# Selective scan in a two-layer Perceiver block: every second unit scans into SBUF, and TensorE turns its states and sums them through diagonals of C

## The reference, cut to what matters

```
ab = seq @ W_in.T
a, g = jnp.split(ab, 2, axis=-1)
...
a = jax.nn.silu(jnp.swapaxes(y, 1, 2))
B = a @ W_sB.T
C = a @ W_sC.T
s_delta = jax.nn.softplus(D_param + a @ W_sD1.T @ W_sD2.T)
expA = jnp.exp(-A_param)
A_bar = expA[None, None] * s_delta[..., None]
X_bar = B[:, :, None, :] * s_delta[..., None] * a[..., None]
...
    h = At * h + Xt
...
out_ssm = jnp.einsum('lbds,lbs->lbd', hid, jnp.moveaxis(C, 1, 0))
out_ssm = jnp.moveaxis(out_ssm, 0, 1) + D_param * a
out = out_ssm * jax.nn.silu(g) @ W_out.T
```

## Time and profile before

| | us |
|---|---|
| median of 3 runs | 764.37 (764.09 to 766.4) |
| the profiled execution, its own time | 763.98 |
| its span in the trace | 761.8 |
| PE busy | 688.7 (90%) |
| DVE busy | 549.7 (72%) |
| POOL busy | 424.2 (56%) |
| ACT busy | 397.0 (52%) |
| first scan to the last chunk's gating | 586.35 to 704.86 |

### The profile page before, as it was taken

How to read it: one execution, slowest core, us unless ns; L and a number is a source line. 1 busy time by engine, 2 the same in 40 slices (tenths; PEclk the granted TensorE clock), 3 DMA queues, 4 the chain that set the end, 5 groups by cost and what they waited for, 6 DMA issues and landing times.

```text
span 761.8 us, 14840 instructions
## 1 busy us (share of the span) xinstructions
PE 688.7 (90%) x5400; PEld 533.1 (70%) x5400; DVE 549.7 (72%) x1182; ACT 397.0 (52%) x754; POOL 424.2 (56%) x448
## 2 busy tenths in 40 slices
PE   5799999999998879999999999998989677678987
PEld 2577777877776668999999999984553222223677
DVE  5678877877878567067777777427474899998586
ACT  3566756656655333466666666432348655432332
POOL 4638634645637025877887777371123779983130
PEclk9999999999999988999999999999999889989999
DMA  8201101101020289999988989989143600001000
GB/s 337 102 2 57 57 1 55 55 0 55 0 93 19 112 322 383 341 374 416 370 317 328 344 336 341 391 320 396 60 145 109 281 0 1 0 0 42 1 1 28
DMA packets 20952, 125.54 MB, mean 165 GB/s; under 512 B 2288, under 2 KB 6784, under 8 KB 13600
## 3 DMA queue, kind: packets, MB, share of 16 engines
q1 hardware_dynamic: 18016, 116.95, 40.2%
q0 software_dynamic: 2880, 7.87, 2.8%
HBM read 114.00 MB, written 10.81 MB: 164 GB/s over the span
## 4 chain that ended last, share of the span: by engine, by line
PE 71%; DVE 17%; ACT 6%; issue 4%; DMA 1%; POOL 0%; SPq 0%; DVEq 0%; ACTq 0%; PEldq 0%
PE banks L1966 61%; PE banks L2035 8%; DVE banks L1844 6%; DVE shown L1855 1%; DMA ctx_raw<-in_ctxT 1%; ACT probs L1019 1%; DVE negmax_raw L1446 1%; PE banks L2203 1%; DVE stats L1333 1%; ACT ctx_hi L1005 1%; DVE xn L1345 1%; DVE X L1925 1%; DVE X L1715 0%; PE banks L2355 0%; ACT banks L1257 0%
## 5 line engine op out<-in xcount | busy, mean ns | idle before, releaser
L1966 PE MATMUL banks<-xT,raw 128*128 128x128 f32 x992 | 150.7, 275 | 0.6 <-DVE xT L1661 0.6
L1966 PEld LDWEIGHTS banks<-xT,raw 128*128 128x128 f32 x992 | 134.5, 191 | 3.3 <-issue 1.1
L891 POOL TENSOR_TENSOR w_lo<-raw,w_hi 128x1024 fp32r<-128x1024 f32 x48 | 113.2, 2384 | 1.7 <-ACT w_hi L1112 1.0
L1143 ACT ACTIVATE banks<-banks,later 128x128 f32<-128x128 f32 x192 | 65.1, 339 | 53.7 <-PE banks L1966 52.3
L955 POOL TENSOR_TENSOR inject<-BCbc,drive 128x1024 f32<-128x1024 f32 x32 | 75.1, 2354 | 29.4 <-DVE banks L1844 15.2
L1966 PE MATMUL banks<-shown,table 128*128 128x512 f32 x128 | 68.7, 667 | 25.0 <-DVE shown L1855 18.5
L1048 ACT ACTIVATE probsT<-banks 128x512 f32<-128x512 f32 x64 | 38.3, 598 | 86.4 <-PE banks L2035 86.1
L1446 DVE TENSOR_REDUCE negmax_raw<-banks 128x1 f32<-128x1024 f32 x64 | 77.6, 1212 | 3.3 <-PE banks L1966 3.2
L1667 DVE CAST mid_hi<-banks 128x128 fp32r<-128x128 f32 x192 | 55.5, 289 | 32.5 <-ACT banks L1143 30.5
L1019 ACT ACTIVATE probs<-banks,negmax 128x1024 f32<-128x1024 f32 x64 | 71.1, 1111 | 10.9 <-DVE negmax L1448 10.8
L1844 DVE TENSOR_TENSOR_SCAN banks<-banks,inject 128x1024 f32<-128x1024 f32 x32 | 73.2, 2289 | 3.2 <-ACT banks L1257 2.5
(11 more groups left out here) (332 smaller groups left out, 1613.9 us busy)
## 6 DMA issues: line engine op xcount, KB each, us to landing
raw<-in_w SPq DMA_DIRECT2D x31, 2048.0 KB, 9.3
ctx_raw<-in_ctxT SPq DMA_DIRECT2D x8, 1024.0 KB, 4.8
ctxT<-in_ctxT SPq DMA_DIRECT2D x4, 2048.0 KB, 9.6
ctxN<-in_ctxN SPq DMA_DIRECT2D x4, 2048.0 KB, 10.8
BCbc<-bc_rows SPq DMA_DIRECT2D x5, 1024.0 KB, 13.5
x_slots<-zero SPq DMA_DIRECT2D x1, 3968.0 KB, 12.1
y_slots<-y_tile POOLq DMA_DIRECT2D x28, 128.0 KB, 7.0
wf<-in_w SPq DMA_DIRECT2D x9, 384.0 KB, 4.8
```

The costliest lines, as they stand in the source:

```text
L891: nc.gpsimd.tensor_tensor(w2_lo[i % WB][:, cols], raw[i % WB][:, EW // 2:][:, cols], w2_hi[i % 2][:, cols].bitcast(F32), ALU.subtract).the ...
L1143: nc.scalar.activation(to, held, ACT.Gelu, bias=b1[:, bass.ds(at + u, 1)]).then_inc(gelu_done, 1)
L1966: return nc.tensor.matmul(o, lhsT, rhs, start=start, stop=stop)
```

## The change

Units with even g stay as they were ("row units"). Units with odd g ("column units", `by_columns`) go another way:

- DVE scans from the PSUM pair and `inject` into `shown[1]` in SBUF, and does not multiply by C. The scan waits until PE has turned the states of the column unit before (`states_turned`).
- PE turns the states (`turn_states`): eight transposes of 128 x 128 into the pair of banks 4 and 5, which the scan has just left.
- ACT copies both banks into `turned_back` (`take_back`), 128 x 512 each; only then may `decays` write the pair for unit n+2 (`states_back`).
- PE sums with C (`sum_columns`): eight fp32 matmuls of 128 x 128, whose stationary operand is the turned states (tokens on partitions) and whose moving operand is a diagonal matrix with C of those 128 tokens. The product turns the states back to channels and weights them.
- The diagonals are made once, in chunk 0 (`build_diag`): 8 products of the identity and a column of C for each of the four odd g, 32 in all, by DVE, into the part of `Cbc` that the odd units no longer load. The columns of C come from four small matmuls of PE behind the first spread rows, copied by DVE (`c_cols`). The first decays wait for that copy, since it frees bank 0.

Around it: the C halves of the odd units' DMAs are gone (4 x 0.5 MB); the three logarithms and the identity scalings on ACT are spread over g = 3 to 6 and POOL's `step_end` waits for its own logarithm alone; the gate keeps two tiles of `gT`; the gate projection stands behind the first column unit's transposes, and `project_out1` behind the second's.

```diff
-        gT = sb("phase", "gT", [P, CC, TOK])
+        gT = sb("phase", "gT", [P, 2, TOK])
+        turned_back = sb("phase", "turned_back", [P, GS, TC, P])
...
+        def by_columns(g):
+
+            return g % 2 == 1
+
+        def c_diag(g, s, t):
+
+            return Cbc[:, GS * g + s, t * P:(t + 1) * P]
...
-                pool.wait_ge(soft_ready, CC)
+                pool.wait_ge(soft_ready, m + 1)
...
-                if n >= 2:
-                    act.wait_ge(shown_ready, n - 1)
+                if n == 0:
+                    act.wait_ge(cols_ready, cols_before + 1)
                 elif n == 1:
                     act.wait_ge(relu_ready, 2)
+                elif by_columns(g):
+                    act.wait_ge(states_back, cols_before + GS * columns_before(n))
+                else:
+                    act.wait_ge(shown_ready, rows_before(n))
...
+            def take_back(n):
+
+                g = n % GROUPS
+                for s in range(GS):
+                    act.wait_ge(states_turned, turned_before + GS * columns_before(n) + s + 1)
+                    if n >= 2:
+                        act.wait_ge(states_used, cols_before + columns_before(n))
+                    nc.scalar.activation(turned_back[:, s].rearrange("p t n -> p (t n)"), pb(2 * HELD_BANKS[g % 2] + s), ACT.Copy)\
+                        .then_inc(states_back, 1)
...
             for m in range(1, CC):
                 for g in range(GROUPS):
+                    if by_columns(g):
+                        take_back(GROUPS * m + g - 2)
                     decays(m, g)
...
+            def build_diag(g):
+                for s in range(GS):
+                    for t in range(TC):
+                        col = NSTATE + GS * g + s
+                        last = nc.vector.tensor_scalar(c_diag(g, s, t), ident, c_cols[:, t, col:col + 1], None, ALU.mult)
+                last.then_inc(diag_built, 1)
...
             step_part(1)
+            dve.wait_ge(cols_done, cols_before + 1)
+            nc.vector.tensor_copy(c_cols[:].rearrange("p t n -> p (t n)"), pb(LOW_BANK)[:, 0:TC * 2 * NSTATE]).then_inc(cols_ready, 1)
             step_part(2)
+            dve.wait_ge(cols_ready, cols_before + 1)
+            build_diag(1)
...
+                    if by_columns(g):
+                        if n >= 2:
+                            dve.wait_ge(states_turned, turned_before + GS * columns_before(n))
+                        nc.vector.tensor_tensor_scan(shown[g % 2][:].rearrange("p g n -> p (g n)"), held, scan_in,
+                                                     0.0, ALU.mult, ALU.add).then_inc(scanned, 1)
+                        if m == 0 and g + 2 < GROUPS:
+                            build_diag(g + 2)
+                        continue
...
+            def turn_states(m, g):
+                n = GROUPS * m + g
+                pe.wait_ge(scanned, n + 1)
+                for s in range(GS):
+                    for t in range(TC):
+                        last = nc.tensor.transpose(pb(2 * HELD_BANKS[g % 2] + s)[:, t * P:(t + 1) * P], shown[g % 2][:, s, t * P:(t + 1) * P], ident)
+                    last.then_inc(states_turned, 1)
+
+            def sum_columns(m, g):
+                n = GROUPS * m + g
+                if m == 0:
+                    pe.wait_ge(diag_built, cols_before + columns_before(n) + 1)
+                for s in range(GS):
+                    pe.wait_ge(states_back, cols_before + GS * columns_before(n) + s + 1)
+                    for t in range(TC):
+                        last = mm(pb(Y_BANK)[:, t * P:(t + 1) * P], turned_back[:, s, t, :], c_diag(g, s, t),
+                                  False, g == GROUPS - 1 and s == GS - 1 and t == TC - 1)
+                last.then_inc(states_used, 1)
...
-                for g in range(GROUPS):
-                    sum_states(m, g)
-                    if g == 1:
+                for g in range(0, GROUPS, 2):
+                    sum_rows(m, g)
+                    turn_states(m, g + 1)
+                    if g == 0:
                         project_gate(m)
-                    if m and g == 3:
+                    if m and g == 2:
                         project_out1(m - 1, False)
+                    sum_columns(m, g + 1)
```

More of the change, by code:

```diff
@@ L1259, in decays @@
                 last.then_inc(decay_ready, 1)
+            def take_back(n):
[6 more added lines that the diff above has]
+                        .then_inc(states_back, 1)
             def silu_g(m):
                 act.wait_ge(gates_done, m + 1)
-                nc.scalar.activation(gT[:, m, :], pb(GATE_BANK), ACT.Silu).then_inc(g_ready, 1)
+                if m >= 2:
+                    act.wait_ge(gated_ready, m - 1)
+                nc.scalar.activation(gT[:, m % 2, :], pb(GATE_BANK), ACT.Silu).then_inc(g_ready, 1)
             def split_high1(n):
@@ L1268, in split_high1, with scale_ident @@
                 nc.scalar.activation(f_hi[n][:], wf[n][:], ACT.Copy).then_inc(f_hi_ready, 1)
+            def scale_ident(m):
+                nc.scalar.activation(skip_diag[:, m * P:(m + 1) * P], ident, ACT.Copy, scale=part(later, LATER, "d_param")[:, m:m + 1])\
+                    .then_inc(skip_made, 1)
             act.wait_ge(expa_ready, 1)
             for g in range(GROUPS):
+                if g >= 3 and by_columns(g - 2):
+                    take_back(g - 2)
                 decays(0, g)
@@ L1282, in _ @@
                         exp_of_step(m)
-                if g == 2:
+                if 3 <= g < 2 + CC:
+                    log_of_step(g - 2)
+                if g == 5:
+                    scale_ident(0)
+                if g == 6:
                     for m in range(1, CC):
-                        log_of_step(m)
-                    for m in range(CC):
-                        nc.scalar.activation(skip_diag[:, m * P:(m + 1) * P], ident, ACT.Copy, scale=part(later, LATER, "d_param")[:, m:m + 1])\
-                            .then_inc(skip_made, 1)
+                        scale_ident(m)
             silu_g(0)
@@ L1296, in _ @@
                         silu_g(m)
+            take_back(UNITS1 - 1)
             act.wait_ge(x_updated, 5)
@@ L1843, in _ @@
                     dve.wait_ge(inject_ready, n + 1)
-                    nc.vector.tensor_tensor_scan(held, held, inject[g % 2][:].rearrange("p g n -> p (g n)"),
-                                                 0.0, ALU.mult, ALU.add).then_inc(scanned, 1)
+                    scan_in = inject[g % 2][:].rearrange("p g n -> p (g n)")
+                    if by_columns(g):
[5 more added lines that the diff above has]
+                            build_diag(g + 2)
+                        continue
+                    nc.vector.tensor_tensor_scan(held, held, scan_in, 0.0, ALU.mult, ALU.add).then_inc(scanned, 1)
                     dve.wait_ge(scanned, n + 1)
@@ L2442, in _ @@
                 spread_row(0, s)
+            pe.wait_ge(low_ready, 1)
+            for t in range(TC):
+                last = mm(pb(LOW_BANK)[:, t * 2 * NSTATE:(t + 1) * 2 * NSTATE], bc[:, t * P:(t + 1) * P], ident[0:2 * NSTATE, 0:2 * NSTATE],
+                          t == 0, t == TC - 1)
+            last.then_inc(cols_done, 1)
             project_step(2)
@@ L2467, in sum_states @@
                 for s in range(GS):
-                    last = mm(pb(Y_BANK), ident, shown[g % 2][:, s, :], g == 0 and s == 0, g == GROUPS - 1 and s == GS - 1)
+                    last = mm(pb(Y_BANK), ident, shown[g % 2][:, s, :], g == 0 and s == 0, False)
                 last.then_inc(shown_used, 1)
+            def turn_states(m, g):
[11 more added lines that the diff above has]
+                    pe.wait_ge(states_back, cols_before + GS * columns_before(n) + s + 1)
+                    for t in range(TC):
+                        last = mm(pb(Y_BANK)[:, t * P:(t + 1) * P], turned_back[:, s, t, :], c_diag(g, s, t),
+                                  False, g == GROUPS - 1 and s == GS - 1 and t == TC - 1)
+                last.then_inc(states_used, 1)
                 if g == GROUPS - 1:
-                    pe.wait_ge(shown_used, GROUPS * (m + 1))
+                    pe.wait_ge(states_used, cols_before + columns_before(n) + 1)
                     pe.sem_inc(y_ready, 1)
```

20 lines of the change are left out of this document (15 added, 5 removed).

## The result

The changed kernel takes 770.54 us (median of 8 runs, 768.05 to 771.6) beside 764.76 for the kernel before on the same chip: ratio 1.0061, 95% interval 1.0037 to 1.0085. It is slower by 0.6%, little but clear of its interval, and the forecast of 757.5 was wrong in sign. The profiled execution took 769.7 us with a span of 767.9, 6.1 us over the 761.8 of before.

The account below looks back on a forecast made before the run. DVE was taken to bound the scan stage, with POOL becoming the bound in chunks 1 and 2. The terms 1.5 - 2.7 + 0.6 - 3.6 - 2.7 + 0.4 = -6.5 us took 763.98 to 757.5 us, range 754 to 763.5.

Parts of the forecast that it names:

- (a): Start of the scan stage: small matmuls and eight diagonals delay the first scan, +1.5 us.
- (b): Chunk 0, first scan to scan 8: products with C and stalls go, diagonals come in, -2.7 us.
- Rival 3: Chunks 1 and 2: POOL's products slow to 2.5 us beside DVE's scans into SBUF, 760; 0.13 together with Rival 2.
- (d): Chunks 1 and 2, scan 9 to scan 25: POOL becomes the bound, a chunk falls from 28.4 to 26.6, -3.6 us.
- Rival 1: Scan stage: TensorE's clock falls, each pair hit adds 3.5 us; one fall (761) 0.08, two or more (764.5, 768) 0.09.
- (c): Scan 8 to scan 9, with chunk 0's gating: the sum now ends late with a column unit, +0.6 us.
- (e): Chunk 3, scan 25 to scan 31: pairs run at 5.68 us plus 1.0 of holds, 18.1 for 20.78, -2.7 us.
- (f): Tail, last scan to the gating's end: about 6.8 us instead of 6.40, +0.4 us.
- Rival 2: PE-ACT-PE handovers each cost 0.3 us more, delaying column scans and chunk-end sums, +3, 760; 0.13 together with Rival 3.
- rival 4: Scan stage: holds fill DVE's saved product in every pair, which stays near 6.9 us, 764 to 766; chance 0.08.

Follow-up runs that it names:

- e3: Changed kernel with all 32 diagonals built ahead of the first scan and POOL's first product held until they are made: 789.21 us, ratio 0.9994 to the kernel before.
- e2: Changed kernel with the eight diagonals of a group built as one two-input product of 128x1024: 780.80 us against 789.02 for the kernel before, ratio 0.9896.
- e9: Changed kernel with each group of diagonals built as two products of 128x512, one per state: ratio 0.9984 to the kernel before.
- e10: Kernel of e2 with the one product for groups 3, 5 and 7 issued later, where POOL's product is already running: ratio 1.0001 to the kernel before.
- e7: Changed kernel with the same 32 diagonal instructions as two-input products instead of products with a scalar: ratio 1.0049 to the kernel before.
- e11: Kernel of e2 with one, two, three weight splits in chunks 1, 2, 3 instead of three each in chunks 1 and 2: ratio 0.9898 to the kernel before.
- e5: Changed kernel itself, run again on another chip: 793.62 us against 789.44 for the kernel before, ratio 1.0047.
- e6: Kernel of e2 with two weight splits in each of chunks 1, 2 and 3 instead of three in chunks 1 and 2: ratio 0.9919 to the kernel before.

## Why the prediction was wrong

**The step that failed is the price of the diagonals**, in (a) and (b): "eight are 1.7 us (1.1 to 2.4)". They took 3.8, 3.7, 4.9 and 3.7. Together 16.2 us instead of 6.8, 9.4 us more, against the 9.3 by which (a) and (b) missed (+8.1 instead of -1.2). The price of one diagonal was right (0.198 in e3). What failed is that I took it from rows in which POOL was idle, issued DMAs or worked on 128x1 (`rstd`, 0.55 us, beside which the 128x256 operation took its 0.41 all the same), for a place where a large product of POOL starts inside every group. The forecast had no term for DVE waiting on POOL there. In its place the runs show an instruction in each group held until POOL's product of 2.35 has ended, 2.4 us instead of 0.27: e3 (POOL idle), e2 (no gap), e9 (one gap) and e10 (whole, but second) show the cause.

The Trainium skill ("SBUF — State Buffer", section "SBUF: two separate sides") states this rule: VectorE and GpSimd share a pair of SBUF ports by "an exclusive lock, not a bandwidth split"; whichever starts first keeps it for its whole instruction, and on VectorE's side this concerns two SBUF inputs (against a GpSimd operation that reads SBUF), or one input in a mode of two ports. The runs agree where they can: 3.42 us for POOL in e2, 3.43 for DVE in e9, two-input products in e7 as much as the one-input ones. No run shows in which mode the one-input diagonals ran. An estimate from the rows at 725 us of the kernel before, where the hold is 2.11 - 0.42 = 1.69 beside a POOL product of 1.84, gives 1.7 + 2.35 - 0.15 = 3.9 for a group that meets one product of POOL; three of the four took 3.7 to 3.8.

Rival 3 asked about POOL and SBUF, but about the scans: "POOL's product takes 2.35 whether DVE scans in PSUM or multiplies into SBUF". That holds: scans and products with one operand in PSUM are not held in any trace here (at most 2.30 and 1.23). It was the wrong evidence for a product that reads SBUF alone.

**(d)** DVE waits for inject, as forecast, and chunk 2 takes 26.77 against 26.6. But that the number came out is in part luck. POOL is busy for 25.74 of the 26.77 us, not without idle time, and e11 has 26.66 with two splits fewer, where the sum of POOL's work gives 23.0. What bounds the chunk is the step and the split at g = 4 together, which two inject buffers don't cover, and not the sum. Chunk 1 missed by 1.8, of which 1.6 is one fall of the clock.

**Rival 1.** I expected no or one fall, and the stage has three. The one in chunk 1 costs 1.6 us, less than half of the price of 3.5 (one short stretch, hidden in part by POOL's time). The two of chunk 0 lie under or beside the held groups and cost nothing that shows: e5, where they fall elsewhere, has the same 34.79. Rival 1 forecast a slower kernel from two falls on; the slower kernel came, but the clock gives only 1.6 of it. And the transposes by themselves don't bring the falls: e6, with the same transposes, has a granted clock of 1.00 from its first scan to its last gating.

**(c), (e), (f)** fell as computed: +0.7 for +0.6; a pair in 5.9 us with holds of 0.20 and 0.36 behind ACT, 17.68 for 18.1; +0.4. Rival 2 (dearer handovers) and rival 4 (no gain in the pairs) are refuted by (e).

**The sum**: -6.5 forecast; +9.3 for the held diagonals, +1.9 in (d), +1.6 ahead of the stage, which the change does not touch, and -0.3 in the rest give +6.0, beside the +6.1 of the spans. Without the hold the change would have been a gain of about the size forecast (0.9%): e2, whose four groups take 5.1 us, 1.3 less than 32 single diagonals at 0.198, is at 0.9896, which makes 0.991, an estimate.

## What to carry to other kernels

Price a small VectorE product or copy on SBUF operands by what GpSimd does at that moment, not by its duration alone: each gap between two such instructions is a place where GpSimd's next product gets in, and the next of them then waits for all of it. Make the run of small instructions one instruction and begin it ahead of GpSimd's. The scans and products with one operand in PSUM were never held here; a diagonal with an operand there was not tried. And when a sum of an engine's work over a stretch hits the measured length, look also at where its work piles up: two splits fewer changed the chunk by 0.1 us. Before costing an edit at a duration from the profile, look at the longest of a group, not only at the mean: a 2.11 among 0.42s was in the trace of the kernel before, and a copy of 1.12 among copies of 0.17.

## What the runs showed that I had not expected

The order of two starts 0.01 us apart decides which engine bears the hold: DVE 2.11 and POOL 1.84 at 724.98, DVE 1.22 and POOL 3.42 at 607.50. And for the same values written, beside one product of POOL, a product made of eight short instructions costs DVE 3.7 to 3.8 us, one made of two costs 3.4, and one whole that begins first 1.2.
